# Where the third expert's weights are loaded, and how many scatters run abreast

## The chip, the cores and the metric

The kernel runs on one core of one Trainium2 chip. The metric is the device time of one execution in microseconds (us), as the median of several runs. The engines are TensorE (PE; its weight loads are PEld), VectorE (DVE), ScalarE (ACT), GpSimd (POOL) and SyncE (SP), which work in parallel and wait for one another by semaphores. DMAs are issued from SP, ACT and POOL.

## The reference

One decoder layer on x of 8 x 256 x 512: self-attention, cross-attention against a context, and a feed-forward part that is a mixture of experts. The change lies in this last part:

```python
E, TOPK, G, TOPK_G, INTER = 16, 4, 4, 2, 352
xt = x.reshape(-1, 512)                                  # 2048 tokens
scores = softmax(xt @ Wg.T)
group_scores = scores.reshape(T, G, E // G).max(axis=-1) # the best 2 of 4 groups stay
topi = top_k(masked, TOPK)                               # 4 experts a token
h = silu(einsum('td,eid->eti', xt, W1)) * einsum('td,eid->eti', xt, W3)
expert_out = einsum('eti,edi->etd', h, W2)
y = einsum('etd,te->td', expert_out, combine)            # weighted sum over a token's experts
z = silu(xt @ Ws1.T) * (xt @ Ws3.T) @ Ws2.T              # shared expert, 2 x 352 wide
return y + z
```

## The kernel before

Tokens stand in 16 tiles of 128. After the two attentions (0 to about 1007 us of the span) come three blocks, each with one program per engine; a block ends for all engines when the last one is done.

**The dispatch block** (`route_and_share`, about 1040 to 1140 us). PE computes the first half of the shared expert, DVE the routing. The routing gives each of a token's four experts a slot in a list of tiles of 128 rows, sorted by expert, in the DRAM array slot_rows. POOL then scatters the rows: 64 indirect DMAs of 256 KB (16 token tiles for each of the 4 choices, a token's lowest-numbered expert first), written in class `Scatters`. Two are in flight: each waits for the one two before it (line 1474). 40 are sent in this block (`EARLY`), 24 in the next. A semaphore `passes` counts finished passes of 16. SP loads the weights of experts 0 and 1, which had been split into fp16 pairs earlier, from we_pairs to fx_w (`first_pairs`, line 1548), and transposes the first two tiles of slot_rows into fx_xt (line 1551).

**The routed block** (`routed_experts`, about 1140 to 1637 us). It runs over the list of tiles, two in a turn. For a tile PE multiplies by the up weights (re_ab, in two halves), transposes the gated result (re_ht_ps, line 1823) and multiplies by the down weights (re_yp). The first half of tile t+1 comes before the transposes and the output of tile t. SP transposes the rows of tile t+2 to fx_xt as soon as tile t has left re_ab (`ab_done`), if the passes it needs are done (line 1743). ACT stores each tile's output into slot_outs. fx_w holds two experts' weights, in slots e % 2. An expert's raw fp32 weights (2.2 MB, loaded in four shares, `load_raw`, line 1761) go to one of two raw buffers: raw_w of this block for even experts, the space of the token rows fx_rows, once all scatters are done, for odd ones. POOL splits them into a high and a low fp16 part: one cast (line 1779) and 16 subtractions (line 1783), and behind every fourth it loads a share of expert e+2 into the place just read. It starts a cast when PE has finished the expert that holds the slot (`y_done`), and tells PE by `w_ready`.

POOL's program at the start of this block, in its order: wait for the pairs, wait for `ab_done` of the first tile, load expert 2's raw weights, the 24 late scatters, wait for them and for the load, load expert 3's raw weights, and then the splits of experts 2 to 15.

**The combine block** (`combine_and_share`, from about 1637 us). POOL gathers the 64 x 128 expert outputs from slot_outs into a ring of 8 buffers (co_yg, line 1932), DVE adds them with their weights, PE computes the second half of the shared expert.

The tiles of routed experts in this input, worked out from the reference's inputs: 4, 4, 4, 5 for experts 0 to 3, and 73 in all.

Of the kernel before, what the change touches and what calls it, by code (L numbers as in the profile page):

```python
# [6 lines left out]
P = 128  # L7
B, S, D = 8, 256, 512
# [1448 lines left out]
class Scatters:  # L1457


    ABREAST, EARLY = 2, 40  # L1460

    def __init__(self, nc, ctx, rows, index, slot_rows):
        self.nc, self.rows, self.index, self.slot_rows = nc, rows, index, slot_rows
        self.sends = [(t, k) for k in reversed(range(TOPK)) for t in range(NT)]
        self.sent = [ctx.enter_context(nc.semaphore(f"sc_sent{n}")) for n in range(self.ABREAST)]
        self.passes = ctx.enter_context(nc.semaphore("sc_passes"))

    def send(self, pool, first, count):
        for m in range(first, count):
            t, k = self.sends[m]  # L1470
            lane = self.sent[m % self.ABREAST]
            if m >= self.ABREAST:
                pool.wait_ge(lane, 16 * (m // self.ABREAST))
            if m >= NT + self.ABREAST - 1 and m % NT == self.ABREAST - 1:
                pool.sem_inc(self.passes, 1)
# [3 lines left out]
            ).then_inc(lane, 16)  # L1479

    def finish(self, pool):
        for lane in self.sent:
            pool.wait_ge(lane, 16 * len(self.sends) // self.ABREAST)
        pool.sem_inc(self.passes, 1)


def route_and_share(nc, split, sems, ident, x_sb, moments, xn, rows, route, wg_dram, we_dram, slot_rows, scatters, first_pairs,
                    xt, x_loaded):


    with ExitStack() as ctx:
# [34 lines left out]
        totals = sb("totals", [P, E, NT + 1], F32)  # L1526
        goes_on = sb("goes_on", [P, E, NT + 1], F32)
# [6 lines left out]
        top = sb("top", [P, NT, 8], F32)  # L1534
        hit = sb("hit", [P, NT, E], F32)
        tile_no = sb("tile_no", [1, TILES], F32)
        passed = sb("passed", [1, TILES, E], F32)
        owner = sb("owner", [1, TILES], F32)
        packed = sb("packed", [1, TILES], F32)
# [14 lines left out]
        def _(pool):  # L1554
# [15 lines left out]
            scatters.send(pool, 0, scatters.EARLY)  # L1570
# [132 lines left out]
def routed_experts(nc, ident, route, we_dram, w, pairs_loaded, rows, xt, x_loaded, scatters, slot_rows, slot_outs, jobs):  # L1703
# [4 lines left out]
    with ExitStack() as ctx:  # L1708
# [5 lines left out]
        raw_w = [sb("raw_w", [P, WC], F32)[:, :],  # L1714
# [43 lines left out]
        def _(pool):  # L1758
# [323 lines left out]
```

## Time and profile before

| | us |
|---|---|
| median of 3 runs | 1756.54 |
| lowest and highest | 1755.86, 1762.98 |
| the profiled execution | 1759.16 |
| its span in the trace | 1757.2 |
| PE busy | 1470.7 (84%) |
| DVE busy | 1037.2 (59%) |
| POOL busy | 695.9 (40%) |
| ACT busy | 620.0 (35%) |

The profile is of one execution; its times count from the start of the span. A line of a timeline has a start, a duration, the engine, the source line, the operation and its tiles; in brackets stands the idle time of the engine before it and who ended it. "PEq" and "POOLq" are the sequencers of these engines. Semaphore and register instructions are not shown as busy. Matmuls are pipelined, and their ends are modelled. The 16 DMA engines are shared by all queues; the DMA share is their mean busy share, and goes above 1 when packets of several queues are outstanding at once.

### The profile page before, as it was taken

The page shows a single profiled execution, that of the slowest core. Times are in us where ns is not written, and L with a number is a line of the kernel's source. Part 1 is how long each engine was busy: PE and PEld are TensorE (multiplying, and loading weights), DVE is VectorE, ACT ScalarE, POOL GpSimd, SP SyncE. Part 2 cuts the span into 40 slices and gives each one's busy share as a digit, 9 for nine tenths or more (in the row PEclk, how much of TensorE's full clock was granted, in tenths as well). Part 3 has the DMA queues.
Part 4 walks back from the last instruction along what each step waited for, and adds up shares of the span by engine and source line. Part 5 has one row for each costly group of instructions (what it writes and reads, how often), then busy time and mean ns, then how long its engine had stood idle before and what let it go on. Part 6 is the DMA issues. An engine that isn't in the chain of part 4 may idle for free. (4 is left out here: it accounts for less than half of the span.)

```text
span 1757.2 us, 28869 instructions
## 1 busy us (share of the span) xinstructions
PE 1470.7 (84%) x9520; PEld 694.4 (40%) x9521; DVE 1037.2 (59%) x1788; ACT 620.0 (35%) x1107; POOL 695.9 (40%) x707
## 2 busy tenths in 40 slices
PE   4689999783878888888888679965999999999987
PEld 2345555441212222222222154432555555556433
DVE  5446465654868879778786575321444545434476
ACT  3232314041366666557666572100111111111211
POOL 1101010035844434434500126436646556656474
PEclk9899999885589999999999969987999999999989
DMA  5853446414632212212110033376565656653465
GB/s 201 265 148 129 111 167 160 162 38 84 194 82 49 52 37 58 45 35 55 31 31 1 25 130 111 140 171 215 144 175 142 177 136 173 174 168 84 136 192 179
DMA packets 197159, 211.25 MB, mean 120 GB/s; under 512 B 90000, under 2 KB 162256, under 8 KB 196688
## 3 DMA queue, kind: packets, MB, share of 16 engines
q1 hardware_dynamic: 167696, 123.67, 26.9%
q0 software_dynamic: 18592, 66.99, 12.5%
q10 hardware_dynamic: 10784, 19.47, 3.1%
q8 instruction: 50, 0.82, 0.2%
q14 instruction: 37, 0.30, 0.1%
HBM read 101.09 MB, written 88.87 MB: 108 GB/s over the span
## 5 line engine op out<-in xcount | busy, mean ns | idle before, releaser
L1035 DVE TENSOR_REDUCE ca_mx<-ca_sc 128x1 f32<-128x512 f32 x512 | 325.4, 676 | 111.1 <-PE ca_sc L947 110.5
L78 PE MATMUL re_ab<-fx_w,fx_xt 128*128 x1800 | 298.5, 317 | 40.3 <-POOLq L1789 21.6
L1177 ACT ACTIVATE ca_pt<-ca_st 128x512 f32<-128x512 f32 x512 | 264.3, 596 | 113.1 <-PE ca_st L959 113.1
L78 PEld LDWEIGHTS re_ab<-fx_w,fx_xt 128*128 128x128 f16 x1800 | 174.5, 99 | 139.9 <-issue 43.1
L947 PE MATMUL ca_sc<-ca_ks,ca_qs 48*128 48x512 f16 x512 | 186.2, 419 | 42.6 <-DMA ca_ks<-ca_scratch 22.9
L959 PE MATMUL ca_st<-ca_qs,ca_ks 49*128 49x512 f16 x512 | 172.4, 396 | 49.1 <-ACT ca_pt L1177 41.3
L78 PE MATMUL re_yp<-fx_w,re_ht 128*128 (+1 forms) x666 | 156.0, 379 | 0.0
L972 PE MATMUL ca_pv<-ca_pt,ca_va 128*32 128x512 f32 x1024 | 143.9, 626 | 1.0 <-DVE ca_turned L1044 0.5
L959 PEld LDWEIGHTS ca_st<-ca_qs,ca_ks 49*128 49x128 f16 x512 | 42.2, 94 | 244.8 <-ACT ca_pt L1177 154.4
L78 PE MATMUL sh_ab<-fx_xn,sh_pair 128*128 (+3 forms) x576 | 130.3, 389 | 3.8 <-PEq L1708 3.3
L1864 ACT ACTIVATE re_gate<-re_ab 128x352 f32<-128x352 f32 x75 | 34.8, 464 | 275.5 <-PE re_ab L78 219.9
L756 POOL TENSOR_TENSOR sa_yt<-sa_yf,sa_yt 128x512 f16<-128x512 f32 x16 | 18.5, 1155 | 252.8 <-ACT sa_yt L690 252.8
L1900 DVE COPY re_ht<-re_ht_ps 128x768 f16<-128x768 f16 x74 | 41.2, 557 | 127.5 <-PE re_ht_ps L1823 126.0
L1241 POOL TENSOR_TENSOR ca_yt<-ca_yf,ca_yt 128x512 f16<-128x512 f32 x32 | 37.0, 1155 | 163.0 <-ACT ca_yt L1166 163.0
L1889 DVE TENSOR_TENSOR re_hf<-re_ab,re_gate 128x352 f32<-128x352 f32 x75 | 39.3, 524 | 104.2 <-PE re_ab L78 102.9
L1891 DVE TENSOR_TENSOR re_hp<-re_hf,re_hp 128x352 f16<-128x352 f32 x75 | 75.1, 1001 | 42.2 <-ACT re_hp L1866 41.6
L1230 POOL TENSOR_TENSOR ca_tf<-ca_tf,home 128x512 f32<-128x512 f32 x32 | 40.6, 1267 | 147.2 <-DVE ca_rf L1030 147.2
L78 PE MATMUL sa_proj<-sa_xn,sa_w 128*128 128x512 f16 x384 | 91.3, 393 | 5.0 <-DVE home L579 3.9
L1866 ACT ACTIVATE re_hp<-re_hf 128x352 f16<-128x352 f32 x75 | 37.2, 496 | 162.6 <-DVE re_hf L1889 160.3
L1932 POOL DMA_INDIRECT co_yg<-slot_outs,fx_index x64 | 71.1, 1112 | 58.3 <-POOLq L1708 28.6
L78 PEld LDWEIGHTS re_yp<-fx_w,re_ht 128*128 128x128 f16 (+1 forms) x666 | 65.1, 98 | 68.9
L78 PEld LDWEIGHTS sh_ab<-fx_xn,sh_pair 128*128 128x128 f16 (+1 forms) x576 | 62.2, 108 | 70.6 <-issue 10.1
(245 smaller groups left out, 2465.1 us busy)
## 6 DMA issues: line engine op xcount, KB each, us to landing
slot_rows<-sa_zeros SPq DMA_DIRECT2D x12, 1792.0 KB, 15.6
slot_outs<-re_ys ACTq DMA_DIRECT2D x74, 256.0 KB, 2.1
re_raw_w<-in_we POOLq DMA_DIRECT2D x28, 544.0 KB
fx_rows<-in_we POOLq DMA_DIRECT2D x28, 544.0 KB, 4.5
sa_scratch<-home SPq DMA_DIRECT2D x16, 512.0 KB, 3.7
ca_scratch<-ca_qk SPq DMA_DIRECT2D x64, 128.0 KB, 1.8
sa_qs<-sa_scratch SPq DMA_DIRECT2D x12, 512.0 KB, 6.6
sa_ks<-sa_scratch SPq DMA_DIRECT2D x12, 512.0 KB, 6.9
```

Source lines behind the costliest of these rows:

```text
L78: last = nc.tensor.matmul(out, lhs(a, c), rhs(b, c), start=(m == 0), stop=(m == total - 1), skip_group_check=parts > 1)
L947: nc.tensor.matmul(sc[:, m % RING, :], qs[rows, c % SLOTS, pair, qt * P:(qt + 1) * P], ks[rows, c % SLOTS, pair, :], start=True, stop=True ...
L959: nc.tensor.matmul(st[:, m % RING, :], ks[rows, b % SLOTS, pair, kt * P:(kt + 1) * P], qs[rows, b % SLOTS, pair, :], start=True, stop=True ...
L972: last = nc.tensor.matmul(pv[j * 32:(j + 1) * 32, :], va[:, b % 2, kt, h, :], pt[:, (4 * qd + j) % 8, :], start=(kt == 0), stop=(kt == 3), ...
L1035: nc.vector.reduce_max(mx[:, qd // 4, qd % 4, 2 * a + jj:2 * a + jj + 1], sc[:, m % RING, :], AX.X).then_inc(maxed, 1)
L1177: nc.scalar.activation(pt[:, (4 * qd + k) % 8, :], st[:, m % RING, :], ACT.Exp, scale=SCALE).then_inc(exp_done, 1)
L1230: nc.gpsimd.tensor_tensor(tf[:, u, :], tf[:, u, :], freq[:, 0, :], ALU.mult).then_inc(rolled, 1)
L1866: nc.scalar.activation(hp[:, s, 0, :], hf[:, s, :], ACT.Copy).then_inc(h_high, 1)
L1889: nc.vector.tensor_tensor(hf[:, s, :], ab[:, s, 1, 0:I], gate[:, s, :], ALU.mult).then_inc(h_ready, 1)
L1891: nc.vector.tensor_tensor(hp[:, s, 1, :], hf[:, s, :], hp[:, s, 0, :], ALU.subtract).then_inc(h_low, 1)
L1900: nc.vector.tensor_copy(ht[:, s, :, :], ht_ps[:, 0:2 * IC, :]).then_inc(ht_ready, 1)
L1932: nc.gpsimd.indirect_dma_start(out=yg[:, m % RING, :], out_offset=None, in_=slot_outs, in_offset=bass.IndirectOffsetOnAxis(ap=route["index ...
```

## The change

The third expert's (expert 2's) raw weights get a tensor of their own, fx_first_raw, which lives through the whole feed-forward part. SP loads them in the dispatch block, in one DMA behind the two pair loads. In the routed block POOL no longer waits for `ab_done` and no longer loads them; fx_first_raw is the raw buffer of all even experts. The late scatters run on four semaphores in place of two, so each waits for the one four before it. The third pass is announced before scatter 51 in place of 49. To make room, eleven small tensors of the routing share one region (scraps), and the gathers' ring lies in fx_rows.

```diff
-    ABREAST, EARLY = 2, 40
+    EARLY, ABREAST_EARLY, ABREAST_LATE = 40, 2, 4
...
-    def send(self, pool, first, count):
+    def send(self, pool, first, count, abreast):
         for m in range(first, count):
             t, k = self.sends[m]
-            lane = self.sent[m % self.ABREAST]
-            if m >= self.ABREAST:
-                pool.wait_ge(lane, 16 * (m // self.ABREAST))
-            if m >= NT + self.ABREAST - 1 and m % NT == self.ABREAST - 1:
+            lane = m % abreast
+            if self.issued[lane]:
+                pool.wait_ge(self.sent[lane], 16 * self.issued[lane])
+            if m >= NT and m % NT == abreast - 1:
                 pool.sem_inc(self.passes, 1)
...
-            ).then_inc(lane, 16)
+            ).then_inc(self.sent[lane], 16)
+            self.issued[lane] += 1
...
-        lg = sb("lg", [P, NT, E], F32)
-        masked = sb("masked", [P, NT, E + TOPK], F32)
-        left = sb("left", [P, NT, E + TOPK], F32)
-        best = sb("best", [P, NT, 8], F32)
+        pieces = (NT * E, NT * (E + TOPK), NT * (E + TOPK), NT * 8, E * (NT + 1), E * (NT + 1))
+        scraps = sb("scraps", [P, sum(pieces)], F32)
+        scrap = lambda n, k: scraps[:, sum(pieces[:n]):sum(pieces[:n + 1])].rearrange("p (a b) -> p a b", b=k)
+        lg, masked, left, best = scrap(0, E), scrap(1, E + TOPK), scrap(2, E + TOPK), scrap(3, 8)
...
             for dram, pair, loaded in first_pairs:
                 sp.dma_start(pair, dram).then_inc(loaded, 16)
+            sp.dma_start(first_raw, we_dram[2]).then_inc(first_pairs[0][2], 16)
...
-            scatters.send(pool, 0, scatters.EARLY)
+            scatters.send(pool, 0, scatters.EARLY, scatters.ABREAST_EARLY)
...
-        raw_w = [sb("raw_w", [P, WC], F32)[:, :],
+        raw_w = [first_raw[:, :],
...
             for e in range(2):
-                pool.wait_ge(pairs_loaded[e], 16)
+                pool.wait_ge(pairs_loaded[e], 16 * (2 - e))
                 pool.sem_inc(w_ready, 1)
-            pool.wait_ge(ab_done, 1)
-            for share in range(LOADS):
-                load_raw(2, share)
-            scatters.send(pool, scatters.EARLY, len(scatters.sends))
+            scatters.send(pool, scatters.EARLY, len(scatters.sends), scatters.ABREAST_LATE)
             scatters.finish(pool)
-            pool.wait_ge(raw_loaded[0], 16 * LOADS)
             for share in range(LOADS):
                 load_raw(3, share)
...
-                pool.wait_ge(raw_loaded[e % 2], 16 * LOADS * (e // 2))
+                if e > 2:
+                    pool.wait_ge(raw_loaded[e % 2], 16 * LOADS * ((e - 1) // 2))
...
-        yg = sb("yg", [P, RING, D], F32)
+        yg = rows[:, 0:RING, :, :].bitcast(F32).rearrange("p r h d -> p r (h d)")
```

POOL's instructions at the start of the routed block, before the change. re_raw_w is the raw buffer, sc_sent0 and sc_sent1 are the two lanes of scatters.

```order
L1757 UNCONDITIONAL_BRANCH [waits barrier_Pool_Activation_PE_DVE_SP_gather]
L1761 DMA re_raw_w<-in_we 128x1088 [waits pairs_loaded0,pairs_loaded1,re_ab_done]
L1761 DMA re_raw_w<-in_we 128x1088 x3
L1476 DMA slot_rows<-fx_rows,fx_index 10752x1024 [waits sc_sent0]
L1476 DMA slot_rows<-fx_rows,fx_index 10752x1024 [waits sc_sent1]
```

And after it, the same place:

```order
L1757 UNCONDITIONAL_BRANCH [waits barrier_Pool_Activation_PE_DVE_SP_gather]
L1477 DMA slot_rows<-fx_rows,fx_index 10752x1024 [waits pairs_loaded0,pairs_loaded1,sc_sent0]
L1477 DMA slot_rows<-fx_rows,fx_index 10752x1024 [waits sc_sent1]
L1477 DMA slot_rows<-fx_rows,fx_index 10752x1024 x2
L1477 DMA slot_rows<-fx_rows,fx_index 10752x1024 [waits sc_sent0]
```

The four loads and the wait for re_ab_done are gone from POOL, the scatters stand first, and the third and fourth of them wait for nothing. SP's instructions in the dispatch block, as the difference between the two:

```order
-L1548 DMA fx_w<-we_pairs 128x8704 x2
+L1547 DMA fx_w<-we_pairs 128x8704 x2
+L1548 DMA fx_first_raw<-in_we 128x4352
 L1551 DMA_TRANSPOSE fx_xt<-slot_rows 128x8x128 [waits sc_passes] x2
```

One DMA more stands on SP, between the pair loads and the first transposes.

## Rows read from the trace of the kernel before

**Rows 1.** The page, parts 1 and 2: busy time; PE's busy tenths in 40 slices.

```profile
PE 1470.7 (84%) x9520; PEld 694.4 (40%) x9521; DVE 1037.2 (59%) x1788; ACT 620.0 (35%) x1107; POOL 695.9 (40%) x707
...
PE   4689999783878888888888679965999999999987
```

**Rows 2.** Who waited for whom: us in total, times, longest us.

```profile
POOL fx_w L1779 <- PE re_yp L78: 134.3, 13, 15.4
...
POOL slot_rows L1476 <- DMA slot_rows<-fx_rows,fx_index: 44.5, 42, 13.6
```

**Rows 3.** Timeline of PE in the routed block: start us, us, engine, line, operation.

```profile
1142.53 7.22 PE L78 MATMUL re_ab<-fx_w,fx_xt 128*128 x36 [3.45 <-issue]
...
1151.88 2.11 PE L78 MATMUL re_yp<-fx_w,re_ht 128*128 x9
1168.30 3.34 PE L78 MATMUL re_ab<-fx_w,fx_xt 128*128 x12 [14.31 <-DMA fx_xt<-slot_rows]
...
1181.40 1.96 PE L78 MATMUL re_ab<-fx_w,fx_xt 128*128 x12
...
1185.32 2.11 PE L78 MATMUL re_yp<-fx_w,re_ht 128*128 x9
...
1202.90 2.11 PE L78 MATMUL re_yp<-fx_w,re_ht 128*128 x9
1226.66 3.70 PE L78 MATMUL re_ab<-fx_w,fx_xt 128*128 x12 [21.64 <-POOLq L1789]
...
1254.17 1.95 PE L78 MATMUL re_ab<-fx_w,fx_xt 128*128 x12
```

**Rows 4.** Timeline of POOL in the same stretch.

```profile
1148.27 2.18 POOL L1761 DMA_DIRECT2D re_raw_w<-in_we  x4 [16.39 <-PE re_ab L78]
1150.75 1.02 POOL L1476 DMA_INDIRECT slot_rows<-fx_rows,fx_index  x1 [0.30 <-issue]
...
1166.65 0.95 POOL L1476 DMA_INDIRECT slot_rows<-fx_rows,fx_index  x1 [13.59 <-DMA slot_rows<-fx_rows,fx_index]
...
1202.43 0.96 POOL L1476 DMA_INDIRECT slot_rows<-fx_rows,fx_index  x1 [0.63 <-DMA slot_rows<-fx_rows,fx_index]
1205.73 2.19 POOL L1761 DMA_DIRECT2D fx_rows<-in_we  x4 [2.34 <-DMA slot_rows<-fx_rows,fx_index]
1208.80 3.81 POOL L1779 CAST fx_w<-re_raw_w 128x4352 f16<-128x4352 f32 x1 [0.88 <-issue]
...
1226.22 0.54 POOL L1761 DMA_DIRECT2D re_raw_w<-in_we  x1 [0.30 <-POOL fx_w L1783]
```

**Rows 5.** Timeline of DVE: its first instruction of the routed block.

```profile
1140.64 0.48 DVE L1885 MEMSET re_ht_ps<- 128x512 f32 x1 [0.83 <-PEq L1491]
```

**Rows 6.** Stretches: us; engines' busy time (instructions); PE clock, DMA share, GB/s.

```profile
1040.40:1053.50 13.10, 12.84 (x50) 5.50 (x51) 11.02 (x70) 4.92 (x7) 3.44 (x8) 0.83 0.85 342
1053.50:1066.90 13.40, 13.40 (x65) 6.68 (x64) 7.49 (x31) 4.29 (x8) 4.96 (x4) 1.00 0.00 1
1166.60:1203.40 36.80, 35.10 (x228) 21.31 (x229) 12.27 (x22) 5.26 (x11) 21.27 (x22) 0.94 0.73 226
1153.10:1166.60 13.50, 0.89 (x5) 0.20 (x2) 1.22 (x2) 0.11 (x1) 0.00 (x0) 0.66 1.20 167
1205.70:1213.50 7.80, 0.00 (x0) 0.00 (x0) 0.14 (x1) 0.00 (x0) 6.80 (x7) 0.69 0.95 318
```

**Rows 7.** Groups by line, POOL, 1166.6 to 1203.5: busy us, mean ns | idle before.

```profile
L1476 POOL DMA_INDIRECT slot_rows<-fx_rows,fx_index x22 | 21.3, 967 | 29.1 <-DMA slot_rows<-fx_rows,fx_index 27.1 <-issue 2.0
```

**Rows 8.** Groups by line, POOL, 1640.6 to 1650 (the combine block's start).

```profile
L1932 POOL DMA_INDIRECT co_yg<-slot_outs,fx_index x8 | 7.9, 992 | 30.7 <-POOLq L1708 28.6 <-issue 2.1
```

**Rows 9.** Timelines of SP, of two short stretches: single transposes.

```profile
1148.92 1.24 SPq L1743 DMA_TRANSPOSE fx_xt<-slot_rows  x1
...
1175.03 0.88 SPq L1743 DMA_TRANSPOSE fx_xt<-slot_rows  x1
```

More of the change, by code:

```diff
@@ L1464, in __init__ @@
         self.sends = [(t, k) for k in reversed(range(TOPK)) for t in range(NT)]
[L1465 removed]
+        self.sent = [ctx.enter_context(nc.semaphore(f"sc_sent{n}")) for n in range(self.ABREAST_LATE)]
         self.passes = ctx.enter_context(nc.semaphore("sc_passes"))
[L1468 removed]
+        self.issued = [0] * self.ABREAST_LATE
+    def send(self, pool, first, count, abreast):
         for m in range(first, count):
             t, k = self.sends[m]
[L1471 to L1474 removed]
+            lane = m % abreast
+            if self.issued[lane]:
+                pool.wait_ge(self.sent[lane], 16 * self.issued[lane])
+            if m >= NT and m % NT == abreast - 1:
                 pool.sem_inc(self.passes, 1)
@@ L1478, in send @@
                 in_=self.rows[:, t, :, :].rearrange("p h d -> p (h d)"), in_offset=None
-            ).then_inc(lane, 16)
+            ).then_inc(self.sent[lane], 16)
+            self.issued[lane] += 1
     def finish(self, pool):
-        for lane in self.sent:
-            pool.wait_ge(lane, 16 * len(self.sends) // self.ABREAST)
+        for lane in range(self.ABREAST_LATE):
+            pool.wait_ge(self.sent[lane], 16 * self.issued[lane])
         pool.sem_inc(self.passes, 1)
 def route_and_share(nc, split, sems, ident, x_sb, moments, xn, rows, route, wg_dram, we_dram, slot_rows, scatters, first_pairs,
-                    xt, x_loaded):
+                    first_raw, xt, x_loaded):
     with ExitStack() as ctx:
@@ L1700, in _, with routed_experts @@
             shared.scalar(act)
-def routed_experts(nc, ident, route, we_dram, w, pairs_loaded, rows, xt, x_loaded, scatters, slot_rows, slot_outs, jobs):
+def routed_experts(nc, ident, route, we_dram, w, pairs_loaded, first_raw, rows, xt, x_loaded, scatters, slot_rows, slot_outs, jobs):
     SHARES, LOADS = 16, 4
@@ L1909, in _, with combine_and_share @@
                 nc.vector.memset(waited[:, 2 * s + 1:2 * s + 2], 0.0)
-def combine_and_share(nc, sems, x_sb, xn, route, we_dram, slot_outs, out_dram, routed):
+def combine_and_share(nc, sems, x_sb, xn, rows, route, we_dram, slot_outs, out_dram, routed):
     RING = 8
@@ L2025, in decoder_block @@
             rows = sf("fx_rows", [P, NT, 2, D], F16)
+            first_raw = sf("fx_first_raw", [P, WC], F32)
             scatters = Scatters(nc, ffn, rows, route["index"], slot_rows)
             route_and_share(nc, split, sems, ident, x_sb, moments, xn, rows, route, a["wg"], a["we"], slot_rows, scatters,
-                            [(we_pairs[e], w[:, e, :, :], pairs_loaded[e]) for e in range(2)], xt, x_loaded)
-            combine_and_share(nc, sems, x_sb, xn, route, a["we"], slot_outs, a["out"],
-                              lambda jobs: routed_experts(nc, ident, route, a["we"], w, pairs_loaded, rows, xt, x_loaded,
+                            [(we_pairs[e], w[:, e, :, :], pairs_loaded[e]) for e in range(2)], first_raw[:, :], xt, x_loaded)
+            combine_and_share(nc, sems, x_sb, xn, rows, route, a["we"], slot_outs, a["out"],
+                              lambda jobs: routed_experts(nc, ident, route, a["we"], w, pairs_loaded, first_raw, rows, xt, x_loaded,
                                                           scatters, slot_rows, slot_outs, jobs))
```

11 lines of the change are left out of this document (4 added, 7 removed).

## The prediction

> **What bounds the kernel now.** I read the page first: TensorE (PE) is busy 84% of the span, and only two of the later slices, the 27th and 28th (1142 to 1230 us), fall to 6 and 5 tenths between nines [rows 1]. Then I read who waited for whom. POOL waited 44.5 us on its own scatters, 13.6 us of it at once, and 134.3 us for PE's output products, 13 times, before a cast of weights [rows 2]. Then the timelines of POOL and PE over that stretch, side by side.
>
> PE starts tile 0 at 1142.53 and is done with what it has at 1153.99 (1151.88 + 2.11). It stands 14.3 us until 1168.30 for the transposed rows of tile 2, works through tile 7, stands 21.6 us from 1205.0 to 1226.66 for expert 2's weights, and from there it hardly stops [rows 3]. A tile takes 5.86 us (outputs 3 and 6 start at 1185.32 and 1202.90) [rows 3]. The second stop ends when POOL has split expert 2: POOL's chain is 16.39 us idle, four load issues, 24 late scatters, four load issues for expert 3, a cast at 1208.80, sixteen subtractions with the last load issue at 1226.22 [rows 4]. So what sets the start of tile 8, and with it everything behind, is POOL's chain from the block's beginning, not PE. The routing, worked out from the reference's inputs, gives experts 0, 1 and 2 four tiles each and expert 3 five, so tile 8 is expert 2's first.
>
> Behind tile 8 PE is the bound: the 13 waits of 134.3 us are POOL's for a weight slot that PE still reads [rows 2]. What tile 8 gains, the end gains.
>
> **The change part by part, on POOL's chain.**
>
> 1. *Wait for PE and four issues go.* The late scatters no longer stand behind ab_done and expert 2's loads. In the new block POOL waits for nothing that is late: pair and raw loads were issued 100 us earlier. DVE's first instruction of the block, released by PE's end of the block before, starts at 1140.64 [rows 5]; I put POOL's first scatter at 1140.7, against 1150.75 [rows 4]. That is 10.0 us, with at most 0.5 us either way.
>
> 2. *Scatters four abreast.* Before, from the first late scatter (1150.75) to the first load of expert 3 (1205.73) it is 54.98 us [rows 4]: two issues and the 13.6 us behind the raw load up to 1166.65 [rows 4], and then 22 in 36.8 us [rows 6], 1.67 us each, of which 0.967 us is the instruction [rows 7]. The rest is the wait for the transfer two before. With four abreast a lane comes round only every fourth. The floor is POOL itself: 0.96 us and 0.30 us between. The first eight gathers of the last block, eight abreast, show it: 0.992 us each and 2.1 us in the seven gaps, a step of 1.29 us [rows 8]. The bounds are 1.29 and 1.67 us. I take 1.29, since a lane's round is then 5.2 us, where two abreast manages on 3.3 us beside PE's traffic. The DMA engines have room: 157 GB/s of the 226 GB/s of that stretch are scatters (22 of 262144 bytes in 36.8 us); at 1.29 us they would be 203, all together 272, and the two pair loads ran at 342 [rows 6]. From the last scatter's start to the load is 3.30 us (1202.43 to 1205.73) [rows 4], and stays. New stretch: 23 x 1.29 + 3.30 = 33.0 us, 22.0 us less. At 1.67 us it is 41.7, 13.3 us less.
>
> 3. *The split stays.* From expert 3's first load issue to the cast 3.07 us, from the cast to PE's start 17.86 us (1208.80 to 1226.66) [rows 3, 4]. The cast then stands at 1140.7 + 33.0 + 3.1 = 1176.8. It also needs expert 0's four tiles done: tile 3's output was over at 1187.4 (1185.32 + 2.11), 19.1 us behind tile 2's start [rows 3], so it now comes at 1153.99 + 19.1 = 1173.1. That is a cover of 3.7 us. Tile 8 starts at 1176.8 + 17.9 = 1194.7, 32.0 us earlier.
>
> 4. *PE's first stop.* The raw load that shared the queue with tile 2's transpose is gone. In the calm stretch a transpose issued at 1175.03 was there for a use at 1181.40, 6.4 us later, without a wait [rows 3, 9]; that bounds it from above. Tile 2's is issued at 1148.92 [rows 9] and wanted at 1153.99, so PE waits 0 to 1.3 us. From there PE needs 36.7 us to tile 8 (1168.30 to 1205.0) [rows 3], 1.4 less if it isn't cold: 1189 to 1192. It is there before POOL, by 3 to 5 us. So the 14.3 us are not a term of the sum beside the 32.0: PE waits for POOL 3 to 5 us instead of 21.6. This is what is late next.
>
> 5. *Clock.* At 1226.66 PE restarts after a long stop: from there to tile 12 at 1254.17 it takes 27.5 us [rows 3], where four tiles of 5.86 make 23.4: 4.1 us lost, mostly at the lower clock. After the short stop of 3.45 us at 1142.53, 36 matmuls took 7.22 us instead of 3 x 1.95 [rows 3], so 1.4 us are lost. A stop of 3 to 5 us I price like that one: at most 4.1 - 1.4 = 2.7 us back. Expert 3's split, 17.9 us like expert 2's [rows 3, 4], starts with tile 7's last product, 6 us into the stretch, and so may end it; that keeps part of the loss. I take 1.5 (0 to 2.7).
>
> 6. *The raw load in the dispatch block.* 2.2 MB more on SP's queue. The two pair loads, 4.5 MB, are done within 1040.4 to 1053.5, and from there to 1066.9, when the scatters begin, the DMA share is 0.00 [rows 6]. The load needs half of 13.1 us, so 6.6 of 13.4 free us. Cost nothing. The first transposes stand behind it on SP but wait for the first scatter pass anyway. If that cover were gone, it would delay POOL's 40 early scatters by at most 6.6 us.
>
> 7. *The rest.* The shared region for the routing's tensors changes names and addresses and no instruction; the gathers' ring in fx_rows waits for what it waited for before. The third pass is announced two scatters later (51 instead of 49), at about 1155, where tile 8 asks for it after 1182. Nothing.
>
> Sum: 10.0 + 22.0 + 1.5 = 33.5 us.
>
> **The rivals.**
>
> *A, the fourth expert's load meets the transposes.* Its four issues leave POOL at 1173.7 and no longer fall in a stop of PE. Tile 7 is due at 1153.99 + 5 x 5.86 = 1183.3, so its transpose is issued some 6.4 us earlier, at 1176.9. Before, the transpose issued at 1148.92, beside such a load, let PE go on only at 1168.30, 19.4 us later [rows 3, 9]; the DMA share was 1.20 at only 167 GB/s [rows 6]. With 19.4 us tile 7 starts at 1196.3 and tile 8, a cold tile later (5.86 + 1.4), at 1203.6: the gain is 23.1 + 1.5 = 24.6 us. Against it: the load is then 3 us old, and such a load alone ran at 318 GB/s and so takes some 7 us [rows 6]; 4 to 5 us of delay cost nothing, since PE would wait for POOL anyway. The Trainium skill ("DMA: Bandwidth & Descriptors", section "SWDGE vs HWDGE vs iDMA") says that POOL's and SP's queues feed different internal queues of the same DMA engines, which serve them in turn. By that rule every transpose issued while a load is queued is slowed, and this rival is the case, with the gain just worked out; the trace agrees in kind (the 19.4 us), and doesn't show how late in a load's life it still holds.
>
> *B, four abreast is no faster.* Something other than the number of lanes sets 1.67 us: gain 10.0 + 13.3 + 1.5 = 24.8 us. For it: the DMA share in that stretch is 0.73 already [rows 6]. Against: the 157 GB/s and the gathers' pace above.
>
> *C, the other side.* Four scatters in flight beside transposes choke as the mix at 1152 to 1167 did, where a scatter held its lane 14.6 us. Four lanes at 14.6 us are 3.65 us per scatter: 23 x 3.65 + 3.3 = 87.3 us, 32 more than before, 10.0 of it made up: 22 us slower, 1779. It decides from 2.68 us per scatter on (23 x 2.68 + 3.3 = 65.0). Against it: from 1166.60 to 1203.40 scatters, transposes and stores ran together without that [rows 6]; the choke stood beside a raw load, which is gone there.
>
> *D, the weights aren't there.* POOL would meet an unfinished raw load. By part 6 it lands 80 us early; excluded but for a per cent.
>
> **How the numbers follow.** The sum is made against the profiled execution: 1759.16 - 33.5 = 1725.7. That execution lies 2.6 us over the median of 1756.54, so the forecast for the median is 1723.0. The chances: forecast 0.68, A 0.14 (1732), B 0.10 (1732), C and other losses 0.04, D or a gain of under 9 us 0.04. The range reaches from 36 us plus some spread of the runs (1718) past A and B with the same spread (1755.86 to 1762.98 before): 1737. Faster by more than 0.5% (8.8 us, about what a measurement of this kernel can tell from no change) 0.92, within 0.5% 0.04, slower 0.04.
>
> **What would show it.** POOL's first late scatter near 1140.7 after the same dispatch block; 24 of them at 1.26 to 1.32 us; the fourth expert's issues near 1173.7, the cast near 1176.8, PE's tile 8 near 1194.7 after a stop of 3 to 5 us; no stop over 1.5 us at tile 2; behind tile 8 the same intervals to the end. A stop of PE at tile 7 or 8 released by the fx_xt load speaks for A, scatter steps over 1.5 us for B, over 2.7 us for C. The prediction is wrong if tile 8 comes sooner and the end doesn't follow.

## The result, and the profile after

The changed kernel took 1742.85 us (median of 4 runs, 1741.75 to 1747.14), the kernel before 1756.49 us beside it (4 runs, 1755.86 to 1762.98). The ratio is 0.9922, with a 95% interval of 0.99 to 0.9944: 13.6 us were gained, where 33.5 were forecast. The profiled execution of the changed kernel took 1747.14 us (span 1745.2), that of before 1759.16. The time lies 5.9 us above the upper end of the range.

The page of the changed kernel, parts 1 and 2, answers to [rows 1]:

```profile
PE 1468.1 (84%) x9520; PEld 692.1 (40%) x9521; DVE 1041.3 (60%) x1788; ACT 620.2 (36%) x1107; POOL 694.0 (40%) x703
...
PE   4689999783878888888888769939999999999887
```

The 28th slice is filled now, from 5 to 9 tenths; the 27th fell from 6 to 3. One stop of PE went and another came. The view of waits (us in total, times, longest us) answers to [rows 2]:

```profile
POOL fx_w L1776 <- PE re_yp L78: 152.7, 14, 20.5
...
DVE re_ht L1897 <- remote: 24.8, 1, 24.8
...
PE re_yp L78 <- DVE re_ht L1897: 23.3, 1, 23.3
...
POOL slot_rows L1477 <- DMA slot_rows<-fx_rows,fx_index: 17.5, 25, 1.3
...
ACT re_gate L1861 <- remote: 15.6, 1, 15.6
```

POOL's wait for its own scatters fell from 44.5 to 17.5 us, its longest from 13.6 to 1.3. Its waits for PE's output products are 14 instead of 13, the new one of 20.5 us. The two rows with "remote" have no counterpart in this block before. The timelines of POOL and PE answer to [rows 3, 4]; POOL first:

```profile
1142.31 0.95 POOL L1477 DMA_INDIRECT slot_rows<-fx_rows,fx_index  x1 [9.98 <-issue]
1143.57 0.96 POOL L1477 DMA_INDIRECT slot_rows<-fx_rows,fx_index  x1 [0.30 <-issue]
...
1171.40 0.96 POOL L1477 DMA_INDIRECT slot_rows<-fx_rows,fx_index  x1 [0.30 <-issue]
1174.89 2.18 POOL L1761 DMA_DIRECT2D fx_rows<-in_we  x4 [2.54 <-DMA slot_rows<-fx_rows,fx_index]
1197.53 3.81 POOL L1776 CAST fx_w<-fx_first_raw 128x4352 f16<-128x4352 f32 x1 [20.45 <-PE re_yp L78]
```

```profile
1143.54 7.23 PE L78 MATMUL re_ab<-fx_w,fx_xt 128*128 x36 [3.41 <-issue]
1150.77 0.51 PE L1820 MATMUL re_ht_ps<-ident,re_hp 128*128 128x128 f16 x6
1151.11 1.95 PE L78 MATMUL re_ab<-fx_w,fx_xt 128*128 x12
1176.33 3.44 PE L78 MATMUL re_yp<-fx_w,re_ht 128*128 x9 [23.27 <-DVE re_ht L1897]
...
1195.24 2.11 PE L78 MATMUL re_yp<-fx_w,re_ht 128*128 x9
...
1215.97 1.96 PE L78 MATMUL re_ab<-fx_w,fx_xt 128*128 x12
```

Up to 1174.89 POOL goes as forecast. The cast of expert 2 then waits 20.45 us for the outputs of expert 0's last tile (1195.24 + 2.11 = 1197.35), since PE stood 23.27 us in tile 0, for a copy by DVE. What DVE and ACT did meanwhile (the first two rows are DVE's, the last two ACT's, from their own timelines):

```profile
1150.18 0.53 DVE L1888 TENSOR_TENSOR re_hp<-re_hf,re_hp 128x352 f16<-128x352 f32 x1 [0.56 <-issue]
1175.52 0.56 DVE L1897 COPY re_ht<-re_ht_ps 128x768 f16<-128x768 f16 x1 [24.81 <-remote]
```

```profile
1149.65 0.50 ACT L1863 ACTIVATE re_hp<-re_hf 128x352 f16<-128x352 f32 x1 [3.19 <-DVE re_hf L1886]
1165.72 0.46 ACT L1861 ACTIVATE re_gate<-re_ab 128x352 f32<-128x352 f32 x1 [15.57 <-remote]
```

PE's transposes for tile 0 (re_ht_ps) stand in the trace at 1150.77, 0.51 us long. DVE copies them at 1175.52, 24.2 us after they ended, and ACT takes the first half of tile 1's products, the last of the 36 matmuls done by 1150.77, at 1165.72, 14.9 us later. Both waited for a semaphore that PE raises. DVE's release came 3.2 us after POOL's last scatter had ended (1171.40 + 0.96); ACT's came while five scatters were still to go. I call this a **held signal**: an engine waits for PE, PE's instruction is over by the trace, and the profile shows no releaser but "remote". (Ends of matmuls are modelled in the trace, so it can't be told from it whether the signal or the product itself was late.) The word "remote" alone isn't enough: every trace of the experiments has such a wait of 8.0 to 8.9 us of DVE sa_mx at about 70 us, far from any indirect DMA. In e13_changed_again that instruction starts 1.14 us behind the first of PE's products for it, and so it does in the result, where the profile names PE. It isn't counted in what follows.

### The profile page after: what moved, and what is told of

It is laid out like the page before. It is cut to its first block and busy times, and to the rows that moved or that the text cites. A ratio compares the mean times of both kernels' runs of the same rounds, so it can differ in the third digit from the quotient of the medians.

```text
span 1745.2 us, 28867 instructions
## 1 busy us (share of the span) xinstructions
PE 1468.1 (84%) x9520; PEld 692.1 (40%) x9521; DVE 1041.3 (60%) x1788; ACT 620.2 (36%) x1107; POOL 694.0 (40%) x703
## 5 line engine op out<-in xcount | busy, mean ns | idle before, releaser
L78 PE MATMUL re_ab<-fx_w,fx_xt 128*128 x1800 | 294.5, 314 | 4.7 <-issue 3.4
L1888 DVE TENSOR_TENSOR re_hp<-re_hf,re_hp 128x352 f16<-128x352 f32 x75 | 78.6, 1048 | 42.2 <-ACT re_hp L1863 41.6
L1929 POOL DMA_INDIRECT fx_rows<-slot_outs,fx_index x64 | 72.3, 1129 | 58.6 <-POOLq L1708 28.6
```

Of the source, the lines that this page charges most:

```text
L78: last = nc.tensor.matmul(out, lhs(a, c), rhs(b, c), start=(m == 0), stop=(m == total - 1), skip_group_check=parts > 1)
L1888: nc.vector.tensor_tensor(hp[:, s, 1, :], hf[:, s, :], hp[:, s, 0, :], ALU.subtract).then_inc(h_low, 1)
L1929: nc.gpsimd.indirect_dma_start(out=yg[:, m % RING, :], out_offset=None, in_=slot_outs, in_offset=bass.IndirectOffsetOnAxis(ap=route["index ...
```

## The experiments

They ran in five studies, each on one chip with the kernel before beside it: chips 10, 6, 13, 9 and 6 again. In the first two I took the chip for indifferent, and so did the expectations; that turned out to be the point. At first there were four theories of the held signals: P, that POOL's issue of indirect DMAs with hardly a pause makes them; F, the fourth lane; T, the transposes on SP's queue; L, the early raw load or the shared region.

### First study, chip 10 (before: 1759.54 us, 18 runs, 1751.03 to 1764.59)

**Late scatters two abreast again**, the rest of the change kept:

```diff
-    EARLY, ABREAST_EARLY, ABREAST_LATE = 40, 2, 4
+    EARLY, ABREAST_EARLY, ABREAST_LATE = 40, 2, 2
```

> The changed kernel with the late scatters two abreast again; the raw load stays in the dispatch block. Theory P (pace): in the changed kernel PE's semaphore increments of tiles 0 and 1 reach ACT, DVE and SP 15 to 25 us late because POOL issues scatters every 1.27 us without ever waiting. Then here, at 1.6 to 1.7 us a scatter with waits between, DVE's re_ht copy of tile 0 starts within 1 us of PE's transposes, PE has no stop at tile 0 or 2 over 2 us, tile 8 starts 61 to 64 us behind the first late scatter, and the time is 1730 to 1735. Theory L (layout or the early load itself): the stop of 23 us at tile 0 stays and the time is 1743 or more.

Measured: 1737.34 us (4 runs, 1733.18 to 1740.2), ratio 0.9864 (0.9829 to 0.99). No remote wait stands in the routed block. The scatters went in steps of 1.80 us, up to 1181.89, and PE stopped only for POOL's split:

```profile
1206.63 3.70 PE L78 MATMUL re_ab<-fx_w,fx_xt 128*128 x12 [18.17 <-POOLq L1786]
```

With half of the change, the early load, the gain against the kernel before was larger (22.2 us) than the result's with the whole (13.6), though on another chip, and the intervals touch at 0.99. L falls, since the early load and the shared region are in this kernel and no signal is held in the routed block; the lanes or the pace are left. In the combine block ACT sh_gate had remote waits here too, 26.2 us in all, the longest 16.7.

**A register load before each late scatter**, four abreast, to slow POOL:

```diff
+            if abreast == self.ABREAST_LATE:
+                pool.value_load(self.ends[0:1, 0:1], min_val=0, max_val=TILES)
```

> The changed kernel, four lanes, with a register load on POOL ahead of each late scatter, which changes nothing in the data. Theory P (pace): the steps grow from 1.27 us to 1.6 us or more, no lane is waited for, and PE's increments come promptly: no stop at tile 0, time 1728 to 1740 by how long the register loads make the stretch. Theory N (lanes): the number of lanes or the missing semaphore waits do the harm, not the step; the stop at tile 0 of over 10 us stays and the time is 1743 or more.

Measured: 1755.18 us (10 runs, 1740.98 to 1764.71), ratio 0.9973 (0.9939 to 1.0006). For 20 of the 23 steps the load hid in the gap and they stayed at 1.27 to 1.30 us (the others up to 2.79, 1.38 on average), so the pace was hardly tried. The held signals stayed (DVE re_ht 15.7 us). The profiled execution, 1744.59 us, is the second fastest of the ten; what made others up to 20 us longer on the same chip stands in no trace.

**Four lanes without the early load**, which stands in the routed block as before:

```diff
-            sp.dma_start(first_raw, we_dram[2]).then_inc(first_pairs[0][2], 16)
...
+            pool.wait_ge(ab_done, 1)
+            for share in range(LOADS):
+                load_raw(2, share)
...
```

> Four lanes for the late scatters, but expert 2's raw weights loaded by POOL in the routed block behind the wait for ab_done, as before. Theory P: the first four scatters are stuck behind the load to about 1166, then some 20 run at 1.27 us, POOL's chain ends 8 to 10 us sooner than before, but PE's increments are late again for 10 to 25 us somewhere from 1170 on; the time is 1750 to 1760. Theory T (the transpose at the beginning of the routed block and four scatters started with it do it): here the scatters start beside the transposes and the load; from 1170 on PE runs undisturbed and the time is 1745 to 1750.

Measured: 1753.34 us (9 runs, 1748.88 to 1762.17), ratio 0.9979 (0.9954 to 1.0003). The signals are held here too, ACT re_gate for 20.1 us and DVE re_ht for 12.8.

**No transposes beside the scatters**: SP waits for the whole scatter before its first transpose of the block.

```diff
+            sp.wait_ge(scatters.passes, TOPK)
```

> The changed kernel; SP waits for the fourth scatter pass before its first transpose of the routed block, so no transpose runs beside the late scatters. PE has to stop at tile 2 until they are done, so the time says nothing and lies near 1745 to 1755. Theory P: ACT's re_gate of tile 1 and DVE's re_ht copy of tile 0 still start more than 5 us behind PE's products. Theory T (a transpose beside POOL's scatters is needed): both start within 1 us.

Measured, in one run: 1753.63 us. The first transpose of the block is issued at 1179.86, behind the last scatter (1175.63), and the waits read

```profile
DVE re_ht L1898 <- remote: 25.2, 1, 25.2
ACT re_gate L1862 <- remote: 15.3, 1, 15.3
```

as in the changed kernel. T falls.

### Second study, chip 6 (before: 1757.32 us, 17 runs, 1752.91 to 1767.36)

**Three lanes** (ABREAST_LATE = 3).

> The changed kernel with three lanes for the late scatters. A lane then comes round after 3.8 us, a scatter holds it for about 2.5 us, so POOL never waits, as with four. Theory P: steps of 1.27 us and a stop of PE of 15 to 25 us at tile 0, as in the changed kernel. Theory F (four lanes or a fourth semaphore do it): no such stop, steps of 1.3 us.

Measured, in one run: 1745.06 us. The steps were 1.27 us for the most part, and DVE re_hf was held 15.7 us, re_ht 9.6, ACT re_gate 6.6. It isn't the fourth lane: F falls.

**44 scatters early instead of 40, all two abreast** (EARLY, ABREAST_EARLY, ABREAST_LATE = 44, 2, 2).

> The changed kernel with two lanes all the way and 44 scatters in the dispatch block, 20 in the routed one: POOL stood idle for some 9 us at the end of the dispatch block. Theory P: no late increments of PE in the routed block; the block boundary stays where PE sets it (within 1 us), tile 8 starts 6 to 7 us sooner than with two lanes and 40, and the time is 1724 to 1732. Rival: the four scatters push the block's end out, and nothing is gained over the 1737 of that version.

Measured: 1734.01 us (5 runs, 1724.76 to 1736.33), ratio 0.9851 (0.9827 to 0.9876). The four go where POOL stood idle, and 20 are left for the routed block. No signal was held there; in the combine block ACT sh_gate was, 5 times for 15.6 us in all.

**The same, and each gather of the combine block waits for the one two before it to land**:

```diff
+                if m >= 2:
+                    pool.wait_ge(fetched[(m - 2) % RING], 16 * ((m - 2) // RING + 1))
```

> The version with 44 early scatters, and in the combine block each gather also waits for the one two before it to land. Theory P says that the first dozen gathers, which go out every 1.3 us without a wait, hold back PE's increments for ACT there too (rows with the releaser remote). Then no ACT sh_gate waits for remote over 1 us in the first 40 us of the combine block, and that block, 118 us from PE's first product to the end before, gets 3 to 10 us shorter. Rival: the gathers get slower, about 1.6 us a step, the block is then bound by 64 of them and is as long as before or longer by up to 5 us.

Measured: 1761.25 us (12 runs, 1756.15 to 1763.76), ratio 1.0013 (0.9996 to 1.0029). ACT sh_gate had no remote wait left; nearly all its idle time (105.6 of 116.3 us) is put down to PE's products. But the gathers became the bound, the last of them late:

```profile
1750.91 0.96 POOL L1931 DMA_INDIRECT fx_rows<-slot_outs,fx_index  x1 [4.16 <-DMA fx_rows<-slot_outs,fx_index]
```

In the kernel without the wait it started at 1717.82. The block took 146.6 us (1613.50 to 1760.1) instead of 116.7 (1617.41 to 1734.1).

**A memset of 0.3 us before each late scatter**, four abreast:

```diff
+                if m > self.EARLY:
+                    pool.wait_ge(self.filled, m - self.EARLY)
+                self.nc.gpsimd.memset(self.filler[:, :], 0.0).then_inc(self.filled, 1)
...
```

> The changed kernel, four lanes, with a small POOL memset of a scratch tensor ahead of each late scatter, so that POOL's step grows while no lane is ever waited for. Theory P (pace): at steps of 1.5 us or more the stop at tile 0 is gone or under 5 us, and the time is 1730 to 1740. Theory N (the missing semaphore waits): the stop of over 10 us stays, and the time is 1743 to 1755.

Measured: 1737.67 us (4 runs, 1734.53 to 1741.72), ratio 0.9881 (0.986 to 0.9902). With steps of 1.43 us the stops of PE are broken up (1.85, 2.86, 0.35 and 9.66 us), and the single waits are shorter than in the result: the longest are 12.0 us (ACT re_gate) and 7.1 (DVE re_ht). There are more of them, though, also of DVE re_hf (7.1 us in all) and re_ys (5.8). By now P looked settled.

### Third study, chip 13 (before: 1755.71 us, 7 runs, 1752.69 to 1756.77)

**Two memsets before each late scatter**, to tell the pace from the waits:

> The changed kernel with two POOL memsets of 128x224 (0.30 us each in the last study) ahead of each late scatter instead of one, still four abreast. The wait on the lane's own scatter is then over when it is asked. Steps about 1.27 + 2 x 0.3 + waits for the memset = 1.75 to 2.1 us, 24 of them 42 to 50 us. This tells the pace from the waits. If it is the pace at which POOL issues (P): no stop of PE's waiters above 3 us in the routed block (no remote wait of DVE re_ht or ACT re_gate above 3 us), PE stops for POOL's split at tile 8 as in the kernel with two lanes; time 1737 to 1747 by POOL's chain. If only a real wait for a transfer lets the signals through (W): remote waits of 10 us and more stay, as with one memset, and the time is no better than 1740. If the lanes (F) were it after all: also holds.

Measured: 1735.42 us (4 runs, 1734.52 to 1738.47), ratio 0.9888 (0.9871 to 0.9904); steps of 1.77 us, no held signal. **Gathers that wait for the fourth before them**, on top of 44 early:

> 44 early scatters and two late lanes as in e6_early_44, and each gather of the combine block waits for the one four before it to land (not two). With two it took all remote waits away but made the gathers the bound (146.6 us for the block instead of 116.7). By P: a gather lands some 4 to 6 us after its issue, so steps become 1.3 to 1.6 us; where they stay below 1.5 the waits for POOL stay partly (sh_gate's remote waits, longest 5.4 us before). If the holds cost time in that block: 1729 to 1732 against 1734 of e6_early_44. If they are hidden there by PE's own queue: 1734, the same. If four are already too few: above 1740.

Measured: 1727.94 us (4 runs, 1722.68 to 1731.56), ratio 0.9854 (0.9837 to 0.9871), no held signal. **The early scatters four abreast as well** (40, 4, 4):

> The changed kernel with the 40 early scatters of the dispatch block four abreast as well. By P: they go out in steps near 1.27 us instead of 1.7 to 1.8, and the shared expert's ACT and DVE operations (sh_gate, sh_h) get remote waits of 5 to 25 us in the dispatch block too; POOL is done with the early scatters about 15 to 20 us before the block ends, but the block itself gets longer or stays. If the hold needs something that only the routed block has (its transposes, its first products): no remote waits in the dispatch block and that block ends at 1139 to 1141 as before. Time 1743 to 1765 by P, 1743 otherwise.

Measured, in one run: 1721.83 us, below both times of the expectation. The 24 late scatters went in steps of 1.27 us, the 40 early ones in 1.32 on average, with 0.30 us between them, and nothing was held anywhere. POOL's rows, and PE's at tile 8:

```profile
1141.12 0.96 POOL L1477 DMA_INDIRECT slot_rows<-fx_rows,fx_index  x1 [21.75 <-issue]
...
1170.23 0.96 POOL L1477 DMA_INDIRECT slot_rows<-fx_rows,fx_index  x1 [0.30 <-issue]
1174.17 2.18 POOL L1761 DMA_DIRECT2D fx_rows<-in_we  x4 [2.98 <-DMA slot_rows<-fx_rows,fx_index]
1176.57 3.81 POOL L1776 CAST fx_w<-fx_first_raw 128x4352 f16<-128x4352 f32 x1 [0.21 <-issue]
```

```profile
1194.60 3.49 PE L78 MATMUL re_ab<-fx_w,fx_xt 128*128 x12 [3.09 <-POOLq L1786]
```

The prediction had the cast at 1176.8, tile 8 at 1194.7 and a stop of 3 to 5 us. More telling still: in this kernel and the one with two memsets the combine block's gathers are not paced, and there too nothing was held, while in the two studies before every kernel with such gathers had it. P as it stood, that the pace alone does it, fell. Left were H, that the hold belongs to the chip (or the execution), and K, that four early lanes take it away.

### Fourth study, chip 9 (before: 1752.81 us, 7 runs, 1747.94 to 1760.64)

**The changed kernel itself:**

> The changed kernel itself, once more. In the last study three kernels with POOL's indirect DMAs in steps of 1.27 to 1.77 us showed no remote wait at all, not even in the combine block, where every kernel of the studies before had them beside the same unpaced gathers. So either the hold belongs to the chip or the execution (theory H: it is there on one chip and not on another, whatever the kernel), or four early lanes took it away (theory K). H, if this chip is of the free kind: no remote waits of ACT re_gate and DVE re_ht, tile 8 at about 1195, 1721 to 1728 us, as the prediction had it. H, if the chip is of the other kind: remote waits of 10 to 25 us here and in the three kernels beside it, 1740 to 1747 us. K: remote waits here, none in the kernel with four early lanes.

Measured: 1724.47 us (4 runs, 1719.81 to 1728.83), ratio 0.9825 (0.978 to 0.987). The same code is 18.4 us faster than in the result, and no signal is held. PE and POOL in its profiled execution:

```profile
1145.84 7.22 PE L78 MATMUL re_ab<-fx_w,fx_xt 128*128 x36 [3.46 <-issue]
...
1155.19 2.11 PE L78 MATMUL re_yp<-fx_w,re_ht 128*128 x9
...
1200.09 3.70 PE L78 MATMUL re_ab<-fx_w,fx_xt 128*128 x12 [7.37 <-POOLq L1786]
```

```profile
1144.57 0.96 POOL L1477 DMA_INDIRECT slot_rows<-fx_rows,fx_index  x1 [9.97 <-issue]
...
1175.00 0.96 POOL L1477 DMA_INDIRECT slot_rows<-fx_rows,fx_index  x1 [0.30 <-issue]
1179.57 2.18 POOL L1761 DMA_DIRECT2D fx_rows<-in_we  x4 [3.61 <-DMA slot_rows<-fx_rows,fx_index]
1181.96 3.81 POOL L1776 CAST fx_w<-fx_first_raw 128x4352 f16<-128x4352 f32 x1 [0.21 <-issue]
```

Tile 0's outputs start at 1155.19, 9.35 us behind the block's first product; in the result it was 32.79. K falls. Beside it **the kernel with 40, 4, 4** again:

> The kernel of e7_early_four once more (40 early scatters four abreast too), beside the changed kernel on one chip. H: it goes as the changed kernel goes, within 3 us: 1721 to 1728 on a free chip, 1740 and more with remote waits in the routed block on the other kind. K: 1721 to 1726 and no remote waits in the routed block, while the changed kernel has them.

Measured: 1722.38 us (4 runs, 1717.6 to 1725.42), ratio 0.9813 (0.9768 to 0.9857): as the changed kernel. And **two late lanes** again:

> The kernel of e1_late_two once more (late scatters two abreast, as before the change), beside the changed kernel. On a chip without holds four abreast are worth what POOL's chain gains, 22.0 - 13.3 = 8.7 us: this one 1731 to 1737, 7 to 11 us slower than the changed kernel. On a chip with holds: 5 us faster than the changed kernel, 1737 as in the first study.

Measured: 1733.42 us (4 runs, 1732.52 to 1735.44), ratio 0.9886 (0.9844 to 0.9927). It is 8.95 us slower than the changed kernel here; by the two values of the prediction's part 2 it should be 8.7. **A candidate, 52 scatters early, all four abreast** (52, 4, 4):

> A candidate: all scatters four abreast and 52 of them in the dispatch block, 12 late. POOL stood 21.8 us idle before the late scatters in e7_early_four; twelve more at 1.27 are 15.2 us of it. Late part: 12 x 1.27 + 3 = 18.2, loads at 1159, and the cast then waits for expert 0's tiles (done at about 1172), so tile 8 starts at 1172 + 18 = 1190 instead of 1194.6, and PE's stop of 3.1 us goes: 2 to 4 us faster than e15_early_four_again without holds (1718 to 1722). With holds in force (other kind of chip): only twelve scatters in a row, so the routed block's holds shrink to under 10 us, and those of the dispatch block come in: 1730 to 1740.

Measured: 1714.26 us (4 runs, 1709.83 to 1718.65), ratio 0.9767 (0.9724 to 0.9809), faster by the medians than the other two (its slowest run and the fastest of 40, 4, 4 overlap by 1.05 us). The cast now waits 11.21 us for PE (at 1175.56), and PE doesn't stop at tile 8.

### Fifth study, chip 6 again (before: 1757.99 us, 10 runs, 1750.11 to 1762.19)

**The changed kernel, a third time:**

> The changed kernel a third time, on whatever chip comes. So far held signals (remote waits of ACT re_gate and DVE re_ht of 6 to 25 us) were seen on the first chip and in the two studies behind it, none in the last two, with the changed kernel at 1742.85 and 1724.47 us. By H (the chip's, whatever the kernel): either remote waits here and 1740 to 1747, or none and 1721 to 1729, and the kernels beside it go the same way. If it is each execution's: times of this one kernel in this study spread over both bands.

Measured: 1745.61 us (7 runs, 1739.51 to 1747.87), ratio 0.9922 (0.9899 to 0.9945), the result's own. The hold is back:

```profile
DVE re_ht L1897 <- remote: 25.6, 1, 25.6
...
PE re_yp L78 <- DVE re_ht L1897: 24.0, 1, 24.0
```

**The candidate:**

> The kernel of e14_early_52 again. By H on a chip without holds: 1714 to 1718, some 10 us below the changed kernel. On a chip with holds: twelve late scatters in a row end at 1158, so that a hold of the routed block ends there, 17 us earlier than the changed kernel's; PE loses 3 to 8 us there and perhaps some in the dispatch block: 1722 to 1735, below the changed kernel by 10 us or more in either case.

Measured: 1779.32 us (4 runs, 1774.05 to 1786.2), ratio 1.0117 (1.0075 to 1.016), 65 us more than on chip 9. Nothing in the expectation was near that. ACT in the dispatch block, and POOL's last early scatter and first late one:

```profile
1078.80 0.63 ACT L1433 ACTIVATE sh_ht<-sh_hf 96x512 f16<-96x512 f32 x1 [0.75 <-issue]
1140.41 0.60 ACT L1428 ACTIVATE sh_gate<-sh_ab 128x512 f32<-128x512 f32 x1 [60.98 <-remote]
```

```profile
1136.58 0.96 POOL L1477 DMA_INDIRECT slot_rows<-fx_rows,fx_index  x1 [0.30 <-issue]
1190.80 0.96 POOL L1477 DMA_INDIRECT slot_rows<-fx_rows,fx_index  x1 [53.26 <-issue]
```

On chip 9 the same instruction of ACT came at

```profile
1092.08 0.60 ACT L1428 ACTIVATE sh_gate<-sh_ab 128x512 f32<-128x512 f32 x1 [14.38 <-PE sh_ab L78]
```

PE began that product at 1086.76 here and at 1086.69 on chip 9, so of the 60.98 us some 48 are late (1140.41 against 1092.08), and the rest ACT waits on either chip. The 52 scatters run without a pause from 1069.69, and ACT goes on 2.9 us after the last has ended. Of the 67.5 us between the two spans (1784.3 and 1716.8) 47.2 stand before the routed block (PE starts at 1192.38, on chip 9 at 1145.23). **The kernel with 44, 2, 2:**

> The kernel of e6_early_44 again (44 early scatters, all two abreast), the fastest on a chip with holds so far (1734.01). On a chip without holds: by POOL's chain 20 late scatters at 1.67 and a start of 1140.7 give 4 x 1.67 = 6.7 us less than with 24 two abreast (1733.42), so 1727 to 1729, 12 to 15 us slower than the 52 early ones four abreast. On a chip with holds: 1731 to 1736, and the question is whether the 52 early ones four abreast are still faster.

Measured: 1729.12 us (4 runs, 1727.3 to 1732.16), ratio 0.9848 (0.9813 to 0.9882). It is 16.5 us faster than the changed kernel on this chip, of which the four moved scatters are 6.7 by the estimate in the expectation.

Medians side by side, in us:

| kernel (early scatters, early and late lanes) | held signals seen | none seen |
|---|---|---|
| before | 1759.54 (chip 10), 1757.32 and 1757.99 (6) | 1755.71 (13), 1752.81 (9) |
| changed (40, 2, 4) | 1742.85 (result), 1745.61 (6) | 1724.47 (9) |
| 40, 2, 2 | 1737.34 (10) | 1733.42 (9) |
| 44, 2, 2 | 1734.01 and 1729.12 (6) | 1727.94 (13, gathers by four) |
| 40, 4, 4 | not run | 1721.83 (13), 1722.38 (9) |
| 52, 4, 4 | 1779.32 (6) | 1714.26 (9) |

H fits all five studies: all kernels of a study go one way, and chip 6 did the same in both of its studies, with the two free ones between them. But only chip 6 was seen twice. That chips 9 and 13 would be free another time wasn't tried, so a cause that comes with the time of a study, and not with the chip, isn't excluded. The changed kernel itself ran on neither chip 10 nor 13. The changed kernel's 7 runs on chip 6 and its 4 on chip 9 don't overlap (from 1739.51 up; to 1728.83). On the chips that hold, P goes with how much, by one traced execution of each kernel: with 24 scatters in steps mostly of 1.27 us the longest remote wait is 15.7 to 25.6 us, with 52 it is 61.0 (some 48 of it late), with steps of 1.43 us 12.0, and with two lanes (steps near 1.8 us, most with a real wait) there is none in the routed block. This comparison stands within chip 10 (e1 against e3, e4 and e5) and within chip 6 (44, 2, 2 against the others). The chip of the result isn't known; its trace has the hold. What differs between the chips isn't known either. In e18_early_52_again PE itself went haltingly for part of the hold, one product at a time with 0.4 to 2.3 us between them from 1094 to 1120, so it may be more than the signal that is late. Whether on a chip that holds it is the pace or the missing wait stays open too: the kernel built to tell the latter ran on a chip without the hold.

## Why the prediction was wrong, and what of it was right

**Part 1** (the wait and four issues go) was right: POOL's first late scatter started at 1142.31 in a block that began 1.01 us later (PE at 1143.54 instead of 1142.53), 9.4 us earlier than before against 10.0 forecast, just outside the 0.5 us either way that it allowed.

**Part 2** (steps of 1.29 us) was right: 23 steps in 29.09 us are 1.265 us each, and from the last start to the load it is 3.49 us (3.30 forecast). On chip 9 it was less good: 23 steps in 30.43 us (1.32 each) and 4.57 us to the load, 20.0 us gained instead of 22.0. Rival B is out: the lanes were what set 1.67 us, as the 8.95 us of e16_late_two_again show. So is C: scatters beside transposes held no lane, the longest wait for one was 1.3 us in the result.

**Part 3** is the step that failed: "That is a cover of 3.7 us". POOL was ready for the cast at 1177.08, but expert 0's tiles, put at 1173.1, were done only at 1197.35, and tile 8 started at 1215.97, not at 1194.7. The loss of 20.45 us at the cast is nearly the whole distance between forecast and result: 19.85 us in the medians (1723.0 and 1742.85), 21.4 in the profiled executions (1725.7 and 1747.14). The timing of tile 3 was carried over from the kernel before, where POOL's scatters had real waits between them; beside unpaused ones DVE's wait for PE's signal was 24.81 us. Where nothing is held, the same step stands: in e13_changed_again the cast followed the load's issue at once (1181.96, 0.21 us idle), and in e7_early_four it was at 1176.57 and tile 8 at 1194.60.

**Part 4** (PE's first stop) was right in what it said of the transpose: no stop at tile 2 in any of the changed kernel's traces, and in the result the stop of 14.31 us [rows 3] gave way to one of 23.27 us just before that place, at tile 0's outputs, for another reason. The stop for POOL of 3 to 5 us was none in the result (PE was later than POOL), 7.37 us in e13_changed_again and 3.09 in e7_early_four.

**Part 5** (1.5 us of clock and what lies behind tile 8): from tile 8 to the end of the span it was 530.5 us before (1226.66 to 1757.2), 529.2 in the result and 526.8 in e13_changed_again; the forecast was 529.0. In the result the clock term shows: up to the combine block's first product it was 410.9 us (1215.97 to 1626.89) instead of 413.3 (1226.66 to 1639.99). In e13_changed_again it was 413.0 (1200.09 to 1613.06), and tile 8's first 12 matmuls took 3.70 us as before [rows 3]: after a stop of 7.37 us this term was 0.4, not 1.5. What that run gained behind tile 8 stands in the combine block, 113.8 us instead of 117.2, which no part of the sum held.

**Part 6** was right. Between 1053.5 and 1066.9 the DMA engines moved 168 GB/s, where before it was 1 GB/s [rows 6], and POOL met no unfinished weights (D). Against **rival A**, the fourth expert's load (1174.89) fell in the end of PE's stop in the result, and in e13_changed_again at 1179.57 beside a working PE: no stop at tile 7. The largest stop for a transpose in the routed block of a kernel with the early load was 5.02 us (e18_early_52_again, beside the fourth expert's load issued at 1208.41), against 14.31 us before (the 19.4 us of the prediction count from the transpose's issue). The rule of queues served in turn (the Trainium skill, "DMA: Bandwidth & Descriptors", section "SWDGE vs HWDGE vs iDMA"), as the prediction applied it, overstated the delay.

Where nothing was held, on chip 9, the changed kernel took 1724.47 us against 1723.0. That this is so near is in part luck. As a gain it is 28.3 us there instead of 33.5, since the kernel before too was faster on that chip, by 3.7 us. Counted from the block's first product, tile 8 came 29.9 us earlier (54.25 us instead of 84.13), where 32.0 were forecast; part 5 gave 0.4 us instead of 1.5. The forecast's ratio, 1723.0 / 1756.54 = 0.981, lies within the measured interval (0.978 to 0.987). So the terms were right in kind and near in size, and the range was too narrow by a condition that it didn't know. The profile of before did hold a hint. The prediction took the step of 1.29 us from the gathers [rows 8], and didn't ask what went on beside them. ACT's timeline of before, in that very block, has the row

```profile
1656.22 0.60 ACT L1428 ACTIVATE sh_gate<-sh_ab 128x512 f32<-128x512 f32 x1 [5.63 <-remote]
```

a signal of PE's held for 5.63 us beside POOL's unpaused gathers. Taken for what it is, it would have been a rival: signals held for up to the whole run of 24 scatters, 23 x 1.29 = 29.7 us, less the cover of 3.7 us, so up to 1723.0 + 26.0 = 1749. The changed kernel's two medians with held signals, 1742.85 and 1745.61, lie under that end. This is worked out after the fact, and it holds for the routed block alone.

## What to carry to other kernels

When a rate is borrowed from another block, read what the other engines did beside it: a pattern that is free where nothing waits for PE's next signal can cost its whole length where something does. Before a faster issue of indirect DMAs is kept, run it on several chips and look for remote waits there. The version that gained most where signals weren't held (0.9767) lost where they were (1.0117), and moving four scatters into POOL's idle time at the old two lanes gave 0.985 on a chip that holds, the best ratio there.

## What the runs showed of the hardware

- Beside unpaused indirect DMAs of POOL, in steps of 1.27 us, other engines went on up to 24 us after PE's product was over by the trace (result), and some 48 us with 52 in a row (chip 6); chip 10 has such waits too. On chips 9 and 13 nearly the same steps (1.27 to 1.32 us), up to 52 in a row on chip 9, delayed nothing. Some holds ended soon after the last of the run: by 3.2 us in the result, 3.9 in e17_changed_third, 4.1 in e5_no_transposes, 2.9 in e18_early_52_again. Others ended in its midst, ACT's in the result with five scatters to go.
- By the Trainium skill ("SBUF — State Buffer", section "Who interferes with whom") the only conflict of engines over SBUF's ports is between DVE and GpSimd, and ACT never waits for one. In this case ACT was held too (re_gate idle for 15.6 us, sh_gate for 61.0), so that conflict by itself doesn't account for the holds. What delays them no run here shows.
- With real waits between the gathers the held signals of the combine block were gone on chip 6 (e8_gathers_paced), at 29.9 us more for the block. Real waits and slower steps came together there, so it doesn't tell them apart.
- Four lanes let POOL issue a scatter every 1.265 us, its own 0.96 us and a gap of 0.30; on chip 9 it was 1.32. With two lanes it was 1.67 us before and 1.77 to 1.86 on average in the experiments.
